# Attention in pairs of units: scores of two, then the values of the two before; four score banks, one value bank, masks behind both scores

## The reference

```python
scores = einsum('bqhd,bkhd->bhqk', q, k) / hd + slopes * (pos_k - pos_q)
scores = where(pos_k <= pos_q, scores, min)        # causal
attn = softmax(scores)
out = einsum('bhqk,bkhd->bqhd', attn, v) @ w_proj + b_proj
x = x + layernorm(out)
```

## Time and profile before

| | us |
|---|---|
| median of three runs | 906.85 (901.68 to 911.57) |
| profiled execution, span | 914.7 |
| attention steps 1 to 8 (from 177.88 to 572.47) | 394.6 |
| one undisturbed step (328.87 to 375.39) | 46.52 |
| PE, DVE, ACT busy over the span | 796.6, 472.7, 390.8 |

### The profile page before, as it was taken

How to read it: one execution, slowest core, us unless ns; L and a number is a source line. 1 busy time by engine, 2 the same in 40 slices (tenths; PEclk the granted TensorE clock), 3 DMA queues, 4 the chain that set the end, 5 groups by cost and what they waited for, 6 DMA issues and landing times. The chain is left out here.

```text
span 914.7 us, 15457 instructions
## 1 busy us (share of the span) xinstructions
PE 796.6 (87%) x4660; PEld 487.6 (53%) x4674; DVE 472.7 (52%) x1161; ACT 390.8 (43%) x714; POOL 239.6 (26%) x202
## 2 busy tenths in 40 slices
PE   4999999679999999999999998769697759999874
PEld 3877876434444444444444433355555647776642
DVE  5544437546455646565556224374747326645066
ACT  5222221136556565656465728244545625344011
POOL 4700022414223232222213011224341540000660
PEclk9999999889999999999999999889898879999987
DMA  9999966454443444434254223342541338983364
GB/s 287 258 280 277 358 169 217 129 125 93 95 94 96 94 96 93 94 85 104 61 126 127 72 87 105 111 139 87 206 156 47 110 81 202 283 215 101 102 211 163
DMA packets 108877, 133.34 MB, mean 146 GB/s; under 512 B 51920, under 2 KB 70992, under 8 KB 107792
## 3 DMA queue, kind: packets, MB, share of 16 engines
q1 hardware_dynamic: 86832, 106.84, 41.9%
q0 software_dynamic: 15728, 19.73, 9.8%
q10 hardware_dynamic: 6256, 6.03, 2.0%
HBM read 84.54 MB, written 50.59 MB: 148 GB/s over the span
## 5 line engine op out<-in xcount | busy, mean ns | idle before, releaser
L972 ACT ACTIVATE probs<-ps,key_bias 128x512 f32<-128x512 f32 (+3 forms) x384 | 201.6, 578 | 161.3 <-PE ps L1640 111.5
L1171 DVE CUSTOM_DVE_ANT_0 ps<-ps,alibi 128x1024 f32<-128x1024 f32 (+7 forms) x256 | 190.9, 779 | 149.0 <-PE ps L1571 145.0
L826 POOL TENSOR_SCALAR alibi<-rel_b,slp 128x1024 f32<-128x1024 f32 x32 | 91.2, 2851 | 317.7 <-DVE rowmax L1171 228.2
L1657 PE MATMUL ps<-probs,ones 128*32 128x512 f32 (+3 forms) x768 | 164.9, 504 | 0.0
L1657 PE MATMUL ps<-probs,v_st 128*32 128x512 f32 (+3 forms) x768 | 164.9, 504 | 0.0
L1571 PE MATMUL ps<-k_st,q_st 96*128 96x512 f32 (+3 forms) x384 | 113.8, 387 | 22.1 <-DVE rowmax L1171 13.8
L1637 PE MATMUL ps<-q_st,k_st 98*128 98x512 f32 (+3 forms) x384 | 126.4, 395 | 7.4 <-ACT probs L972 3.6
L1571 PEld LDWEIGHTS ps<-k_st,q_st 96*128 96x128 f32 x384 | 63.6, 192 | 114.2 <-DVE rowmax L1171 83.2
L1637 PEld LDWEIGHTS ps<-q_st,k_st 98*128 98x128 f32 x384 | 72.0, 196 | 44.9 <-ACT probs L972 31.3
L1780 PE MATMUL ps<-xsT,w13r 128*128 128x256 bf16 (+1 forms) x552 | 67.8, 280 | 10.1 <-DMA xsT<-rows_by_expert 10.1
L1780 PEld LDWEIGHTS ps<-xsT,w13r 128*128 (+1 forms) x552 | 58.0, 108 | 22.3 <-issue 11.7
(11 more groups left out here) (181 smaller groups left out, 1189.6 us busy)
## 6 DMA issues: line engine op xcount, KB each, us to landing
qk_split<-qk_out SPq DMA_DIRECT2D x32, 512.0 KB, 8.5
q_st<-qk_split SPq DMA_DIRECT2D x48, 256.0 KB, 4.5
k_st<-qk_split SPq DMA_DIRECT2D x48, 256.0 KB, 6.5
results_by_tile<-ro ACTq DMA_DIRECT2D x23, 256.0 KB, 4.3
w13r<-in_w POOLq DMA_DIRECT2D x16, 352.0 KB, 34.4
x_a<-in_x SPq DMA_DIRECT2D x4, 1024.0 KB, 8.4
v_rows<-v_out SPq DMA_DIRECT2D x16, 256.0 KB, 3.9
v_st<-v_rows SPq DMA_DIRECT2D x16, 256.0 KB, 7.1
```

The costliest lines, as they stand in the source:

```text
L826: pool.tensor_scalar(alibi[h % 2][:, :], rel_b[:, :], slp[par][:, h:h + 1], None, ALU.mult).then_inc(b_alibi, 1)
L972: act.activation(probs[:, v % 3, e, 0:width], ps[:, score_bank(v, e), 0:width], ACT.Exp, bias=key_bias[par][:, 2 * pair + e, j - 4 * qc + ...
L1171: dve.tensor_tensor_reduce(scores, scores, alibi[h % 2][:, S - width:S], 1.0, -3e38, ALU.add, ALU.max, rowmax[:, h, i:i + 1]).then_inc(b_m ...
L1657: last = pe.matmul(ps[row:row + HD, 6 + g % 2, q0 - CH * qc:CH], lhsT, probs[:, v % 3, e, 0:width], start=j == 0, stop=j == 4 * qc + 3, ti ...
```

## The change

PE now works in 12 **batches** of two units: scores of units 2b and 2b + 1, then the values of units 2b - 2 and 2b - 1. The values of a step's last two units run in batch 0 of the next step. Scores have four banks (3 to 6), values one (7), `probs` four slots. The masks of both heads stand behind both heads' scores. The maxima are dealt out by a table, MAX_PER_BATCH: one ahead of the first scores, one between the two, the rest behind them, none in the last three batches. The shifts' transpose stands in batch 9 behind its first scores. ACT's copy of the fourth group stands behind the first two units of the next step. In SBUF `probs` grows by 4 KB, and buffers of later stages trade places (not shown).

```diff
-MAX_END = 0.79
...
+BATCHES = NS // 2
+MAX_PER_BATCH = [3, 4, 3, 4, 4, 4, 3, 4, 3, 0, 0, 0]
+MAX_AT = [range(sum(MAX_PER_BATCH[:b]), sum(MAX_PER_BATCH[:b + 1])) for b in range(BATCHES)]
+MAX_BY = max(b for b in range(BATCHES) if MAX_PER_BATCH[b])
+SHIFT_AT = MAX_BY + 1
...
 def score_bank(v, e):
-    return 3 + (2 * v + e) % 3
...
-PROJ_AT = [6, 7, 9, 10]
+    return 3 + 2 * (v % 2) + e
+
+
+VALUE_BANK = 7
+INVERT_AT = 4
+
+
+PROJ_AT = [3, 4, 5, 6]
 ROOTS_AT = [17, 22]
-MAX_BY = 1 + max(v for v in range(NS) if MAX_AT[v])
...
-            probs = place(a, "probs", [P, 3, 2, CH], F32)
+            probs = place(a, "probs", [P, 4, 2, CH], F32)
...
-                    if e == 0 and not (v < 3 and isinstance(it, int) and it == 0):
-                        act.wait_ge(b_pv, it * NS + (v - 2))
-                    act.activation(probs[:, v % 3, e, 0:width], ps[:, score_bank(v, e), 0:width], ACT.Exp,
+                    if e == 0 and not (v < 4 and isinstance(it, int) and it == 0):
+                        act.wait_ge(b_pv, it * NS + (v - 3))
+                    act.activation(probs[:, v % 4, e, 0:width], ps[:, score_bank(v, e), 0:width], ACT.Exp,
...
-                act.copy(raw[:, g // 2, g % 2, :], ps[:, 6 + g % 2, :]).then_inc(b_raw, 1)
+                act.copy(raw[:, g // 2, g % 2, :], ps[:, VALUE_BANK, :]).then_inc(b_raw, 1)
...
                     exps(it - 1, 1 - par, v)
+                    if v == 1 and not (isinstance(it, int) and it == 1):
+                        copy_out(it - 2, 3)
                     if v - 2 in GROUP_END:
                         copy_out(it - 1, GROUP_END[v - 2])
-                    if v == MAX_BY + 1 and maxima:
+                    if v == 2 * SHIFT_AT and maxima:
                         shift_rows(it)
-                copy_out(it - 1, 3)
...
-                for v in range(NS):
-                    if v == 8 and not (isinstance(it, int) and it < 2):
+                for b in range(BATCHES):
+                    if b == INVERT_AT and not (isinstance(it, int) and it < 2):
                         invert_sums(it - 2)
-                    for u in MAX_AT[v]:
+                    for u in MAX_AT[b]:
                         row_max(it, u)
-                    if v == MAX_BY:
+                    if b == MAX_BY:
                         shifts(it, par)
...
-                    if not (2 * v + e < 3 and isinstance(it, int) and it == 0):
-                        pe.wait_ge(b_exp, (it * NS + v) * 2 + e - 2)
+                    if not (v < 2 and isinstance(it, int) and it == 0):
+                        pe.wait_ge(b_exp, (it * NS + v) * 2 + e - 3)
                     last = pe.matmul(ps[:, score_bank(v, e), 0:width], k_st[par][0:98, h, j * P:(j + 1) * P],
                                      q_st[par][0:98, h, q0:q0 + width], start=True, stop=P * j != q0)
-                    if P * j == q0:
-                        last = pe.matmul(ps[:, score_bank(v, e), 0:P], identb[:, :], future[:, :],
-                                         start=False, stop=True)
-                    last.then_inc(b_st, 1)
+                    if P * j != q0:
+                        last.then_inc(b_st, 1)
+                if P * j == q0:
+                    for e in range(2):
+                        pe.matmul(ps[:, score_bank(v, e), 0:P], identb[:, :], future[:, :],
+                                  start=False, stop=True).then_inc(b_st, 1)
...
-                if j == 0 and not (g < 2 and isinstance(it, int) and it == 0):
-                    pe.wait_ge(b_raw, it * 4 + (g - 1))
+                if j == 0 and not (g == 0 and isinstance(it, int) and it == 0):
+                    pe.wait_ge(b_raw, it * 4 + g)
...
+                for b in range(BATCHES):
+                    units = MAX_AT[b] if maxima else ()
+                    if not maxima and b in PROJ_AT:
+                        project_first(PROJ_AT.index(b))
+                    max_at(b, units[0:1])
+                    scores_of(it - 1, 2 * b, 1 - par)
+                    if maxima and b == SHIFT_AT:
+                        transpose_shifts(it)
+                    max_at(b, units[1:2])
+                    scores_of(it - 1, 2 * b + 1, 1 - par)
+                    max_at(b, units[2:])
+                    if b:
+                        if b == 1:
+                            pe.wait_ge(b_vin[1 - par], 32 * (n + par))
+                        for v in (2 * b - 2, 2 * b - 1):
+                            values_of(it - 1, v, 1 - par)
+                    elif not (isinstance(it, int) and it == 1):
+                        for v in (NS - 2, NS - 1):
+                            values_of(it - 2, v, par)
```

More of the change, by code:

```diff
@@ L116 @@
 NS, NM = len(SCORE_UNITS), len(MAX_UNITS)
-MAX_END = 0.79
-def spread_maxima():
-    work = [min(CH, CH * (qc + 1) - P * j) for _, qc, j in SCORE_UNITS]
-    cost = [P * (i + 1) + P for _, i in MAX_UNITS]
-    done, at, u = 0, [], 0
-    for v in range(NS):
-        share = sum(cost) * min(1, sum(work[:v + 1]) / (MAX_END * sum(work)))
-        first = u
-        while u < NM and done + cost[u] / 2 <= share:
-            done, u = done + cost[u], u + 1
-        at.append(range(first, u))
-    assert u == NM
-    return at
+BATCHES = NS // 2
[3 more added lines that the diff above has]
+SHIFT_AT = MAX_BY + 1
+assert sum(MAX_PER_BATCH) == NM
 MAX_FROM = 12 - NM // DC
@@ L311, in build @@
             recips = place(a, "recips", [P, HD], F32)
-            place(a, "clear_of_b", [P, 7360], F32)
+            place(a, "clear_of_b", [P, 6336], F32)
             alibi = [alibi0, place(a, "alibi1", [P, S], F32)]
@@ L370, in build @@
             g_c = place(a, "g_c", [P, MT, CH], F32)
-            silu = place(a, "silu", [P, 2, CH], F32)
+            g_lo = place(a, "g_lo", [P, MT, CH], F32R)
             logT_c = place(a, "logT_c", [P, CH], F32)
-            ring = [place(a, "ring0", [P, D], BF16)]
+            ring = [place(a, f"ring{n}", [P, D], BF16) for n in range(RING - 1)]
             place(a, "to_hole", [P, 240], F32)
@@ L380, in build @@
             g_hi = place(a, "g_hi", [P, MT, CH], F32R)
-            g_lo = place(a, "g_lo", [P, MT, CH], F32R)
-            ring += [place(a, f"ring{n}", [P, D], BF16) for n in range(1, RING)]
+            silu = place(a, "silu", [P, 2, CH], F32)
+            ring.append(place(a, f"ring{RING - 1}", [P, D], BF16))
         with ExitStack() as a:
@@ L387, in build @@
             s2_raw = place(a, "s2_raw", [P, MT, D], F32)
-            place(a, "past_lists", [P, 2456], F32)
+            place(a, "past_lists", [P, 2416], F32)
             with ExitStack() as t:
@@ L394, in build @@
             gin_hi = [place(a, f"gin_hi{n}", [P, MT, CH], F32R) for n in range(CHUNKS - 1)]
-            gin_lo = [place(a, f"gin_lo{n}", [P, MT, CH], F32R) for n in range(CHUNKS - 1)]
-            place(a, "past_gin", [P, 456], F32)
+            gin_lo = [place(a, f"gin_lo{n}", [P, MT, CH], F32R) for n in range(CHUNKS - 2)]
+            place(a, "past_g_lo", [P, 2032], F32)
             s2_hi = place(a, "s2_hi", [P, MT, D], F32R)
@@ L399, in build @@
             sil = place(a, "sil", [P, 4, TS], F32)
+            gin_lo.append(place(a, f"gin_lo{CHUNKS - 2}", [P, MT, CH], F32R))
         gin_hi.append(g_hi)
@@ L1656, in values_of @@
                                       (64 + HD * e, ones[:, :])):
-                        last = pe.matmul(ps[row:row + HD, 6 + g % 2, q0 - CH * qc:CH], lhsT,
-                                         probs[:, v % 3, e, 0:width], start=j == 0,
+                        last = pe.matmul(ps[row:row + HD, VALUE_BANK, q0 - CH * qc:CH], lhsT,
+                                         probs[:, v % 4, e, 0:width], start=j == 0,
                                          stop=j == 4 * qc + 3, tile_position=(0, row))
@@ L1689, in pe_step, with max_at @@
                 pe.wait_ge(b_rows, 32 * it)
[L1690 to L1707 removed]
+                def max_at(b, units):
+                    for u in units:
+                        if u == 0:
+                            pe.wait_ge(b_in[par][0], 6 * 16 * (n + 1))
+                        if u == NM // 2:
+                            pe.wait_ge(b_in[par][1], 6 * 16 * (n + 1))
+                        max_scores(it, u, par)
+                for b in range(BATCHES):
[5 more added lines that the diff above has]
+                    if maxima and b == SHIFT_AT:
+                        transpose_shifts(it)
+                    max_at(b, units[1:2])
[9 more added lines that the diff above has]
+                            values_of(it - 2, v, par)
             transpose_shifts(0)
@@ L1715, in _ @@
             pe_step(STEPS, 0, STEPS // 2, maxima=False)
+            for v in (NS - 2, NS - 1):
+                values_of(STEPS - 1, v, 1)
             pe.wait_ge(b_raw, 4 * STEPS)
```

22 lines of the change are left out of this document (2 added, 20 removed).

## The result

The changed kernel takes 920.88 us (median of four runs, 919.71 to 922.12), the kernel before 906.34 beside it (901.68 to 911.57): 1.015 times as long, 95% interval 1.0116 to 1.0184. The forecast was 919 us, slower. The total came out; several of its terms did not.

What follows compares the result with a forecast made beforehand. PE bounds a step (busy 44.8 of 46.5 us). Terms 6.6 + 0.5 + 1.2 + 4.5 = 12.8 us on a profiled 914.7 give 927.5; that execution was 7.85 above the median, so 919 us, range 899 to 934.

Steps and rivals of the forecast that it cites:

- PE's work in a step, pairs and masks: Attention steps: fewer seams between kinds of matmul save 3.1 us of PE work a step, bounds 1.7 and 4.4.
- waits on row maxima in a step: Clustered maxima in batches 0, 1, 3, 5 and 7: PE waits 4.1 us a step for DVE, 1.7 before.
- wait at the transpose: Shifts' transpose behind the last maximum: PE waits 1.3 us, as DVE's shifts come later than PE's work ends.
- values of unit 4 behind the sums: Unit 4's values wait for ACT's first copy, held by later sums: 0.5 us a step, bounds 0 and 1.8.
- step 1: First attention step: first maximum ahead of first score, two values units leave; 0.5 us more.
- steps 2 to 7, clock included: Middle attention steps: 1.1 us more each, 6.6 in all, plus 3.0 for two more stretches at 1.2 GHz.
- last step, to its second copy, clock included: Later fourth-group copy delays the first projection to 13.1 us into the step: +1.2, plus 1.5 for low clock.
- The seven stops of the walk: PE's predicted waits for units 0, 4, 8, 10, 18, 24 and 26 in the new order, 4.1 us a step.
- Masked pairs under 0.6 us: Sign in PE's timeline: masked pairs taking less than 0.6 us would make the kernel even or faster.
- Faster: Rival: DVE keeps pace and waits stay at 1.7 us; a step loses 3.1 us, time 888; chance 0.16.
- Even: Rival: seams at their upper bound, 4.4 us less a step, no further low-clock stretch; time 909; chance 0.27.
- Much slower: Rival: sums land later, unit 4 waits 1.8 us, low clock in nearly every step; time 933; chance 0.11.

Runs made afterwards that it cites:

- narrowed kernels: Kernel before and changed kernel, in each of which VectorE reads only the last 128 columns of a maximum; 894.38 and 891.32 us.
- n_after: Changed kernel, with VectorE reading only the last 128 columns of each maximum; 891.32 us in one run.
- e3_sums: Changed kernel, with the second pair's sums stored ahead of the next heads' loads on SP's queue; 915.49 us, 1.0102 of the kernel before.
- e3_even_sums: Changed kernel with maxima dealt 3,3,3,3,3,3,3,3,4,4, transpose in batch 10 and sums stored ahead of the loads; 890.64 us, 0.983 of before.
- e2_even: Changed kernel with maxima dealt 3,3,3,3,3,3,3,3,4,4 and the transpose in batch 10; 919.78 us, 1.0128 of before.
- n_before: Kernel before, with VectorE reading only the last 128 columns of each maximum; 894.38 us in one run.
- e6_even_masks: e3_even_sums with each mask behind its own head's scores again; 896.19 us, 0.9879 of before.
- e9_best: e3_even_sums with last step's values of units 22 and 23 and ACT's fourth-group copy ahead of first scores and exponentials; 887.64 us, 0.9808 of before.
- e10_proj: e9_best with the four pieces of the first projection one batch later each; 881.41 us, 0.9732 of before.

## Why the prediction was right, and where only by chance

| term | predicted | measured |
|---|---|---|
| PE's work in a step, pairs and masks | -3.1 (-1.7 to -4.4) | -3.6 (narrowed kernels) |
| of it, masks | -0.5 (-1.0 and +0.5) | -0.7 before, -0.3 in the pairs |
| waits on row maxima in a step | from 1.7 to 4.1 | from 1.7 to 3.1 or 3.4 as listed, six places |
| wait at the transpose | 1.3 | 1.0 to 1.1 (0.3 in step 7) |
| values of unit 4 behind the sums | 0.5 (0 to 1.8) | 0.2 to 1.3 |
| undisturbed step | 47.6 | 46.9 to 47.7 (45.7 in step 7) |
| step 1 | +0.5 | +4.9 |
| steps 2 to 7, clock included | +9.6 | +2.2 |
| last step, to its second copy, clock included | +2.7 | +4.1 |
| sum | +12.8 | +14.1 at the first expert |

**Right:** the mechanism of the step. Pairs save PE's work, and the maxima's stops, the transpose and the sums eat it. The places were the ones named: six of the seven holds of a bank (of units 0, 4, 8, 10, 18 and 26; the smallest, of unit 24, is too short for a row of the waits), the transpose in batch 9, unit 4 for the sums. The data chain of the last step came out at 13.2 us for 13.1. Taking the forecast from the median and not from the profiled execution was right too: the 7.85 us were in the tail behind the experts (9.7 us, as a timed run is 1.8 us longer than its span: 920.99 and 919.2 for the changed kernel).

**Nearly right, the waits.** As listed they are 5.1 us for 5.9 predicted, and 41.1 us of work and 5.1 of waits make 46.2, not the 47.35 of the step. The rest is stops too. A bracket begins at the modelled end of the row ahead, and short stops have none. From start to start, a mask and the maximum behind it lie 0.94 us apart in the changed kernel and 0.10 in the narrowed one, so this stop costs 0.84 us where its bracket says 0.65 (first the changed kernel, then n_after):

```profile
288.56 0.29 PE L1635 MATMUL ps<-future,identb 128*128 128x128 bf16 x2
289.50 0.68 PE L1563 MATMUL ps<-k_st,q_st 96*128 96x512 f32 x2 [0.65 <-DVE rowmax L1163]
```

```profile
277.51 0.29 PE L1635 MATMUL ps<-future,identb 128*128 128x128 bf16 x2
277.61 0.65 PE L1563 MATMUL ps<-k_st,q_st 96*128 96x512 f32 x2
```

Over the step the distances ahead of maxima are 4.5 us longer than in n_after, 3.4 of it listed; all others agree within 0.02 us for each kind of neighbours, but for the waits at unit 4 and the transpose. So no matmul is slower, and 41.1 + 4.5 + 1.1 + 0.6 is the step. The seven stops of the walk are 4.1 of the 4.5, just its sum, unit 24's 0.26 among them (3.7 in every other step, where unit 0's is shorter). That GpSimd's table makes the shifts slow, as the prediction has it, is not settled: in the profile of before they took 1.44 us where a table begins just behind their start and 0.64 with no table beside them (509.95), but also 0.63 in the middle of one (173.45).

**Wrong, the clock in the steps.** Two more stretches at 1.2 GHz were expected and one fewer came: one step of six under 1.00, where before had two. That is about half of the 7.4 us by which steps 2 to 7 were forecast too long; the other half is that at full clock steps 2 to 6 lost about 0.75 us each, not 1.1, and step 7 gained 0.9. The rows support only that a stretch can begin at a wait of 0.9 to 3.3 us. Whether it does, the same wait of 0.92 us answers with no step of six in the changed kernel and five of six in e3_sums. The section of the Trainium skill that the prediction weighed ("TensorE: Matmul & The Clock Gate", "HAM oscillation — how this bites in real kernels") counts only longer pauses; by that rule e3_sums would have no such step, so the trace does not bear it out. The next section of that page of the Trainium skill ("A second HAM failure mode: psum-queue depth-cycling") tells of a clock that moves to and fro where PE pauses only shortly between groups of matmuls, and gives no length for the pauses; the falls behind 0.92 us in e3_sums are in keeping with it. A term of 3.0 us with the sign of a coin should have stood in the range, not in the sum.

**Wrong, step 1.** The 0.5 us were worked out from the order of PE's instructions at full speed. Missed was that the clock is low when the keys come, and that in step 1 the values, behind which it rose in every trace, now stand a batch later: 9.5 us more at half speed in this profile, 6 to 7 in those of the other kernels with pairs. The key wait is in the profile of before; the earlier trace rows begin behind it, and nothing in the prediction looked at the clock there.

**Wrong, one sign to look for.** Masked pairs under 0.6 us were to make the kernel even or faster. In PE's timeline of the changed kernel two masked scores of 512 columns start 0.56 us ahead of the next maximum (the 0.81 us before ran up to values), and the kernel is slower: the saving was not what decided.

```profile
287.44 0.62 PE L1629 MATMUL ps<-q_st,k_st 98*128 98x512 f32 x2
...
288.00 0.31 PE L1563 MATMUL ps<-k_st,q_st 96*128 96x128 f32 x1
```

**The rivals.** *Faster* was said to fail on how long a bank is held. e3_even_sums has the same holds and in listed waits loses only 1.4 to 1.8 us to them: the spacing of the maxima decides, not the hold. *Even* asked for seams at their upper bound and no further stretch at the low clock. The first came most of the way (3.6 of 4.4 us saved in a step) and the second in full for steps 2 to 7 (one stretch fewer), and the kernel is slower all the same, since step 1 and the last step cost 9 us where 3 were allowed. *Much slower* rested on the sums at their bound of 1.8 us with a low clock in each step. e2_even shows just that mechanism, with 2.1 to 3.3 us: it was there, and the changed kernel's stops ahead of unit 4 kept it small.

So the sum was right by chance: +4.4 in step 1, +1.4 in the last step and +3.0 in rows of the first table that the prediction had at nothing (0.7, 1.2 and 1.1) stood against -7.4 in steps 2 to 7.

## What to carry to other kernels

A saving on the engine that bounds a loop arrives only up to the next fixed moment in it: look for the event with a time of its own (here sums that land 6 us behind a store, queued behind loads that nobody needed yet) and move that first; the same even spread of maxima, beside the kernel with the later transpose alone, cost 6 us before that move and gave 15 after it. When work is grouped, deal out again what was interleaved with it, and check the first and the last pass of the loop by themselves, since deferred work falls out of the one and into the other. Two wrong terms can make a right sum, so compare the stages of two profiles before believing it.

## What the runs showed of the hardware

From the rise in step 1 to the end of step 7, every fall of the clock in the 14 traces stands at a wait of PE of 0.92 to 3.3 us, in it or up to 1.4 us behind it. In the five kernels whose longest wait in steps 2 to 7 is 0.66 us or less (n_before, e3_even_sums, e6_even_masks, e9_best, e10_proj) there is no fall in these steps. A wait of 0.92 us does not always bring it: the clock fell in the same place of every step from step 2 to step 6 in e3_sums, behind 0.92 us, and not once there in the changed kernel, which has the same wait. Taking a wait of 0.2 to 1.3 us out of each step so gained e3_sums nothing from step 2 to step 8 (284.9 us for 284.4). And PE stayed at 1.2 GHz for 14.3 us of which it worked 13.95, on scores, masks and maxima until the last 5.4. In 14 traces of this stage the rise to 2.4 GHz came 2.4 to 5.5 us behind the first values matmuls.
